# Pacing indirect transfers with a longer memset instead of tile gates, and a table that places the attention mix

## The reference

```python
x = x + 0.5 * ffn(layernorm(x))      # mixture of 8 experts, 2 chosen for each token
x = x + attention(layernorm(x))      # RWKV time mix: token shift, k, v, r, a scan over the sequence, Wo
x = x + 0.5 * ffn(layernorm(x))      # the same experts again
```

## Time and profile before

| | us |
|---|---|
| median of 3 runs | 674.68 (673.13 to 674.70) |
| the profiled execution | 672.78 |
| its span, first to last instruction | 671.0 |

### The profile page before, as it was taken

The page is one execution under the profiler, slowest core; times in us unless marked ns, Lnnn a source line. Parts: engine busy times, 40 slices in busy tenths (PEclk is TensorE's granted clock), DMA queues, the critical chain, the costliest instruction groups (busy, mean ns, idle before and its releaser), DMA issues. The chain is left out here.

```text
span 671.0 us, 18790 instructions
## 1 busy us (share of the span) xinstructions
PE 528.1 (79%) x5866; PEld 482.5 (72%) x5866; DVE 412.7 (62%) x1218; ACT 319.7 (48%) x703; POOL 297.2 (44%) x499
## 2 busy tenths in 40 slices
PE   2136899993899889898999859989789999989500
PEld 1125799893788878677888749878789899879500
DVE  4845975221678789588897848859786443333311
ACT  5433754441484566654656615854645344334100
POOL 1270356666540550565405655046005555525543
PEclk9999999998799999998999959999799999999955
DMA  8943234442221221222211133111112324322311
GB/s 287 325 143 99 84 112 147 136 134 67 76 77 41 64 72 49 73 64 63 78 49 45 53 99 83 44 60 49 57 34 77 100 81 127 85 64 72 86 52 43
DMA packets 89016, 59.57 MB, mean 89 GB/s; under 512 B 10208, under 2 KB 82656, under 8 KB 88928
## 3 DMA queue, kind: packets, MB, share of 16 engines
q1 hardware_dynamic: 55248, 29.97, 15.3%
q0 software_dynamic: 8192, 16.79, 8.9%
q10 hardware_dynamic: 25488, 11.61, 5.9%
HBM read 28.65 MB, written 29.69 MB: 87 GB/s over the span
## 5 line engine op out<-in xcount | busy, mean ns | idle before, releaser
L694 POOL DMA_INDIRECT rows_in<-parts,slot x128 | 132.5, 1035 | 232.9 <-DVE h L1084 136.4
L1084 DVE TENSOR_TENSOR h<-sil,pb 128x512 f32<-128x512 f32 x177 | 120.9, 686 | 145.8 <-PE pb L1201 59.3
L1215 PE MATMUL py<-ffn_w,h 128*128 x1416 | 199.0, 284 | 13.6 <-ACT yrow L753 12.4
L1215 PEld LDWEIGHTS py<-ffn_w,h 128*128 128x128 f32 x1416 | 175.3, 195 | 20.0 <-issue 13.9
L1201 PE MATMUL pa<-rT,ffn_w 128*128 128x128 f16 (+1 forms) x1752 | 152.7, 234 | 36.8 <-DVE h L1084 26.0
L708 POOL DMA_INDIRECT yg<-rows_out,slot x128 | 123.8, 968 | 130.3 <-issue 53.6
L1201 PEld LDWEIGHTS pa<-rT,ffn_w 128*128 x1752 | 124.9, 100 | 52.6 <-issue 41.1
L1201 PE MATMUL pb<-rT,ffn_w 128*128 128x128 f16 (+1 forms) x1752 | 157.1, 233 | 0.1
L1201 PEld LDWEIGHTS pb<-rT,ffn_w 128*128 x1752 | 124.4, 99 | 7.6 <-issue 0.3
L768 ACT ACTIVATE sil<-pa 128x512 f32<-128x512 f32 x177 | 105.4, 595 | 42.6 <-PE pa L1201 32.8
L748 ACT ACTIVATE rT<-pT 128x512 f16<-128x512 f16 (+1 forms) x112 | 56.8, 508 | 92.5 <-PE pT L1188 81.2
(11 more groups left out here) (155 smaller groups left out, 442.0 us busy)
## 6 DMA issues: line engine op xcount, KB each, us to landing
rows_out<-yrow ACTq DMA_DIRECT2D x177, 64.0 KB
rin<-rows_in SPq DMA_DIRECT2D x65, 128.0 KB
rows_in<-zrow SPq DMA_DIRECT2D x34, 128.0 KB
shared<-in_w SPq DMA_DIRECT2D x16, 256.0 KB, 7.0
rin<-rows_in SPq DMA_DIRECT2D x47, 64.0 KB
rows_in<-zrow SPq DMA_DIRECT2D x2, 1472.0 KB, 12.2
xres<-in_x SPq DMA_DIRECT2D x4, 512.0 KB, 5.7
ffn_w<-in_w SPq DMA_DIRECT2D x8, 256.0 KB
```

The costliest lines, as they stand in the source:

```text
L694: pool.indirect_dma_start(rows_in[g][:], bass.IndirectOffsetOnAxis(ap=slot[:, c, at:at + 1], axis=0), parts[:, at, :], None).then_inc(s_sc ...
L1084: dve.tensor_tensor(h[:, t % RING, :], sil[:, t % 2, :], pb[t % 2][:], ALU.mult).then_inc(s_h, 1)
L1215: mm = pe.matmul(py[:], h[:, step % RING, at:at + T], w, start=(c == 0), stop=(c == FC - 1))
```

## The change

1. **Pacing.** The list of transfers loses its gates (`s_h`). The memset behind each grows from 64 to 544 bytes a partition, into one of four buffers in turn; it waits only for the memset four transfers back, and the next transfer waits for no memset at all.
2. **Gather buffers by order.** `yg` has 3 buffers, used in the order of the gathers; a gather of unit n waits for the combine of the gather three before it.
3. **The last unit by blocks.** The 2 gathers of each of the last unit's 4 blocks have a semaphore of their own; DVE combines a block when both are there, and SP stores each block by itself.
4. **Placement.** The planner's costs change a little (`LAND` 4.0 to 4.5, `UP` 0.67 to 0.66 or 0.73, the slips), `SPACE` stays 1.6. A table `NOT_BEFORE` gives 36 steps a first tile, and `DUE_SHIFT` moves three due times.

```diff
-PACE = 64
+PACE = 544
+PACES = 4
+GSLOTS = 3
...
-HOP, LAND, SEND, LOAD = 0.1, 4.0, 1.1, 3.0
-SLIP = {"dve": 6.0, "act": 3.1, "pe": 2.0}
+HOP, LAND, SEND, LOAD = 0.1, 4.5, 1.1, 3.0
+SLIP = {"dve": 6.2, "act": 2.6, "pe": 2.0}
 SPACE = 1.6
+DUE_SHIFT = {
+    "stats6.1": -4, "combine2.0": -2, "stats5.0": 30
+}
+NOT_BEFORE = {
+    "stats2.0": 2, "pick21.0": 5, "hi2.0": 7, "rsqrt3.1": 7, "place21.0": 9, "hi3.1": 12, "xnT2.0": 12,
+    "pick22.0": 19, "scatter2.0": 23, "keep3.1": 27, "combine0.0": 35, "att0.0": 48, "v0.1": 48, "hi4.0": 59,
+    "xnT4.0": 61, "mstats1.1": 64, "count4.0": 66, "mnorm1.1": 68, "xT1.1": 71, "hi_m2.1": 90, "out2.0": 99,
+    "att2.1": 106, "combine3.0": 106, "mstats3.0": 107, "combine3.1": 112, "count6.0": 118, "turn_m3.1": 121,
+    "peak3.1": 126, "r3.1": 127, "exps3.1": 129, "scatter7.0": 133, "divide3.1": 134, "divide23.1": 135,
+    "stats8.0": 138, "turn8.0": 142, "combine4.1": 148, "combine5.0": 163
+}
...
-        if any(t is None for t in times):
+        if any(t is None for t in times) or tile < NOT_BEFORE.get(f'{step}{c.run}.{c.unit}', EARLY):
             return None
...
-            sp.wait_ge(s_out, 16 * B)
+            sp.wait_ge(s_out, 16 * (B - 1 + JU))
...
-                    before = [p[1:] for p in PLAN if p[1] == "gather" and p[3] == b]
-                    at_b = before.index(("gather", run, b))
-                    if at_b:
-                        pool.wait_ge(s_comb, count(("combine",), ("combine", before[at_b - 1][1], b)))
+                n = GATHERS.index((run, b))
+                if (j, c) == (0, 0) and n >= GSLOTS:
+                    pool.wait_ge(s_comb, count(("combine",), ("combine", *GATHERS[n - GSLOTS])))
...
-            for sent, (gate, name, *one) in enumerate(TRANSFERS):
-                wait(pool, s_h, gate)
-                wait(pool, s_pace, sent)
+            for sent, (_, name, *one) in enumerate(TRANSFERS):
                 if name == "scatter":
                     scatter(*one)
                 else:
                     gather(*one)
-                pool.memset(pace[:], 0).then_inc(s_pace, 1)
+                wait(pool, s_pace, sent - PACES + 1)
+                pool.memset(pace[:, sent % PACES, :], 0).then_inc(s_pace, 1)
...
+            def combine_last(run, b):
+
+                u, js = units(run, b)
+                slot_ = (len(GATHERS) - 1) % GSLOTS
+                for j in range(JU):
+                    xj = xres[:, js, :][:, j, :]
+                    dve.wait_ge(s_last[j], 16 * TOPK)
+                    for c in range(TOPK):
+                        ins = dve.scalar_tensor_tensor(xj, yg[:, slot_, c, j, :],
+                                                       wts[:, c, u * JU + j:u * JU + j + 1], xj, ALU.mult, ALU.add)
+                        if c == 0:
+                            link(ins)
+                    ins.then_inc(s_lastc, 1)
```

More of the change, by code:

```diff
@@ L157, in __init__ @@
     def __init__(self, steps, run, unit, due, start, follows=()):
-        self.steps, self.run, self.unit, self.due, self.start = steps, run, unit, due, start
+        self.steps, self.run, self.unit, self.start = steps, run, unit, start
+        self.due = (due[0] + DUE_SHIFT.get(f'{steps[0]}{run}.{unit}', 0),) + due[1:]
         self.follows, self.ends = list(follows), {}
@@ L187, in tile @@
         q, half, _ = TILE_OF[t]
-        up1 = max(self.free["pe"], self.rT[q] + HOP, self.h.get(t - 2, 0.0) + HOP) + UP
+        up = UP if paired(t) else UP_ALONE
+        up1 = max(self.free["pe"], self.rT[q] + HOP, self.h.get(t - 2, 0.0) + HOP) + up
         if t > SKEW:
@@ L191, in tile @@
         turned = self.turn(q + 1, up1) if t + 1 < TILES and TILE_OF[t + 1][1] == 0 else up1
-        up3 = turned + UP
+        up3 = turned + up
         silu = max(self.free["act"], up1 + HOP) + SILU
@@ L311, in ask, with in_use @@
         waiting.append([due, at, name, run, [(b, j, c) for b in units for j in range(JU) for c in range(TOPK)]])
+    def in_use(run, unit):
+        order = [p[2:] for p in plan if p[1] == "gather"]
+        n = order.index((run, unit))
+        return n >= GSLOTS and "combine" not in gathered[order[n - GSLOTS]].ends
     def send(tile, until):
         while True:
-            now = [w for w in waiting if w[1] <= until and not (w[2] == "gather" and any(
-                c.next() == "combine" for c in chains if c.unit == w[4][0][0] and gathered.get((c.run, c.unit)) is c
-                and c.run < w[3]))]
+            now = [w for w in waiting if w[1] <= until and not (w[2] == "gather" and in_use(w[3], w[4][0][0]))]
             at = max([free["pool"]] + [min((w[1] for w in now), default=until)])
@@ L385, in count @@
     return order.index(upto) + 1
+GATHERS = [p[2:] for p in PLAN if p[1] == "gather"]
 def run_of(t):
@@ L445, in macaron_kernel @@
         zrow = sb("zrow", [P, 2 * D], F16)
-        pace = sb("pace", [P, PACE], U8)
+        pace = sb("pace", [P, PACES, PACE], U8)
         e_desc = sb("e_desc", [P, JG, E])
@@ L490, in macaron_kernel @@
         yrow = sb("yrow", [P, YSLOTS, D])
-        yg = sb("yg", [P, UG, TOPK, JU, D])
+        yg = sb("yg", [P, GSLOTS, TOPK, JU, D])
         qkv_f = yg[:].rearrange("p b c j d -> p (b c j) d")[:, 0:6, :]
@@ L558, in macaron_kernel @@
         s_yst = [sem(f"y_stored{i}") for i in range(YSLOTS)]
-        s_gat = [sem(f"gathered{b}") for b in range(UG)]
+        s_gat = [sem(f"gathered{i}") for i in range(GSLOTS)]
+        s_last = [sem(f"last_gathered{j}") for j in range(JU)]
+        s_lastc = sem("last_combined")
         s_comb = sem("combined")
@@ L649, in step @@
                     u, js = units(run, b)
+                    if (run, b) == GATHERS[-1]:
+                        for j in range(JU):
+                            sp.wait_ge(s_lastc, j + 1)
+                            sp.dma_start(ov[:, js, :][:, j, :], xres[:, js, :][:, j, :]).then_inc(s_out, 16)
+                        return
                     sp.wait_ge(s_comb, count(("combine",), ("combine", run, b)))
@@ L702, in gather @@
                         pool.wait_ge(s_yst[k], 16 * len(range(k, PEND[run], YSLOTS)))
-                if (j, c) == (0, 0):
-                    before = [p[1:] for p in PLAN if p[1] == "gather" and p[3] == b]
-                    at_b = before.index(("gather", run, b))
-                    if at_b:
-                        pool.wait_ge(s_comb, count(("combine",), ("combine", before[at_b - 1][1], b)))
+                n = GATHERS.index((run, b))
+                if (j, c) == (0, 0) and n >= GSLOTS:
+                    pool.wait_ge(s_comb, count(("combine",), ("combine", *GATHERS[n - GSLOTS])))
                 pool.indirect_dma_start(
-                    yg[:, b, c, j, :], None, rows_out[SET[run]][0:PASS_STEPS[PASS[run]] * T, :],
-                    bass.IndirectOffsetOnAxis(ap=slot[:, c, at:at + 1], axis=0)).then_inc(s_gat[b], 16)
+                    yg[:, n % GSLOTS, c, j, :], None, rows_out[SET[run]][0:PASS_STEPS[PASS[run]] * T, :],
+                    bass.IndirectOffsetOnAxis(ap=slot[:, c, at:at + 1], axis=0)).then_inc(
+                        s_last[j] if n + 1 == len(GATHERS) else s_gat[n % GSLOTS], 16)
             def every(run, units):
@@ L1088, in combine @@
                 u, js = units(run, b)
-                runs = [p[2] for p in PLAN if p[1] == "gather" and p[3] == b]
-                dve.wait_ge(s_gat[b], 16 * TOPK * JU * (runs.index(run) + 1))
+                n = GATHERS.index((run, b))
+                dve.wait_ge(s_gat[n % GSLOTS], 16 * TOPK * JU * (n // GSLOTS + 1))
                 for c in range(TOPK):
@@ L1093, in combine @@
                         xj = xres[:, js, :][:, j, :]
-                        ins = dve.scalar_tensor_tensor(xj, yg[:, b, c, j, :], wts[:, c, u * JU + j:u * JU + j + 1],
-                                                       xj, ALU.mult, ALU.add)
+                        ins = dve.scalar_tensor_tensor(xj, yg[:, n % GSLOTS, c, j, :],
+                                                       wts[:, c, u * JU + j:u * JU + j + 1], xj, ALU.mult, ALU.add)
                     if c == 0:
@@ L1106, in step @@
                 if name == "combine":
-                    combine(run, b)
+                    (combine_last if (run, b) == GATHERS[-1] else combine)(run, b)
                 if name in ("stats", "mstats"):
```

2 lines of the change are left out of this document (1 added, 1 removed).

## The result

The changed kernel takes 626.87 us in the median of 4 runs (625.27 to 627.24), beside 674.69 for the kernel before on the same chip: a ratio of 0.929 (95% interval 0.926 to 0.931), 47.8 us less. The profiled execution took 627.05 us, its span 625.2, so 45.8 us less than the span before. The forecast was 641, the range 626 to 668: the sign was right, the gain was four tenths larger than the sum, and the time lies 0.9 us inside the lower edge of the range.

A forecast was written before the change was run, and what follows sets the result against it. The prediction took POOL's transfer spacing to bound the first combine and the end. Its terms (-11.5, -2, -1.5, -2.5, -2, -4, -10.0) summed to -33.5 us: 639.3 profiled, 641.2 against the median; range 626 to 668.

The forecast's parts named there:

- Spacing: POOL's paced transfers: without the wait for the memset they start 1.75 us apart, with a memset of 0.44 to 0.54 us.
- The gates: Tile gates on POOL's transfers: hardly binding; 1 to 3 us at the tail, 1.2 counted in the tail's spacing.
- The first combine: DVE's 13.1 us wait at the combine of run 0, unit 0 falls to about 1.6: -11.5 us.
- What is late next: Run 2's rows, ready at 186.4 and needed at 188: covered with 2 us to spare, but not at spacing 1.9.
- Other waits in the body and run 5: Gather waits in the body -1.5, -2.5 and -2 us; PE's 4.08 us wait for run 5's rows, -4 us.
- The tables at 0, 8 either way: Table moves of mix and routing steps remove no instruction: counted at 0, possibly 8 us either way.
- The tail: From run 6's first gather: spacing -8.0 us, fewer combines behind the last gather -1.6, smaller store -0.4; together -10.0.
- (3): Rival: spacing above the tiles' rate, POOL falls behind everywhere; at 2.4 us +19, so 694; chance 0.10.
- (2): Rival: the memset hides in the issue, spacing 1.4 us; -49.5 us, so 625; chance 0.10.
- (1): Rival: the body gives less, transfers stretched to a mean of 1.9 us; -17, so 657.7; chance 0.22.
- (4): Rival: held-back table steps come due together before runs 4 to 7, DVE stalls PE; +30, about 675; chance 0.10.
- (5): Rival: the longer memset delays DVE's single-input mix instructions; 3.4 us, at most 12: 645 to 653; chance 0.08.

The follow-up runs named there:

- run 6: Not a follow-up run but a stretch of the kernel's own work; its first gather starts at 601.76 us in the kernel before. It has no measured time or ratio.

## Why the prediction was right, and where its terms were off

The places named, the first combine, the waits in the body, run 5 and the tail, are those where the time was won, and the lead cause, POOL's spacing, is the right one. The size of the whole is not: the sum was 33.5 us, measured were 47.8. That the range holds the time, by 0.9 us, is luck. Its lower end stood for a memset hidden in the issue, at 1.4 us of spacing, and that did not come.

*Spacing*: 1.75 forecast, 1.69 measured. The memset took 573 ns (forecast 0.44 to 0.54 us, by a line through three short ones), the gap ahead of a transfer 0.16 us and not 0.30. The two errors partly cancel.

*The gates*: put at 1.2 us; in the changed kernel they cost 13. This was the worst step. It read the gates' price from a plan in which they stood close to their data (0.9 us behind it at run 5), and carried it to a plan in which they stand up to 9.95 us behind. What the gates cost in the order before, no run shows: pacing alone takes away gates, spacing and the wait for the memset together.

*The first combine*: -11.5 forecast, -2 more for the clock and -1.5 for the second combine; both waits and the low clock are gone, and the stretches from tile 34 to 46 give 17.2 together. The reason given, the order of the list, is one of two that nearly suffice: the order with the old pacing leaves a wait of 4.3 us, the new pacing with the old order 1.7.

*What is late next*: run 2's rows were to be ready with 2 us to spare at 1.75 and late at 1.9. They never were late in a kernel without gates, not even at 1.88. The step took the scatters to start at tile 23, since the table says so; they started at 119.17, as soon as their slots were made. In the changed kernel with the old pacing they were 0.7 us late.

*Other waits in the body and run 5*: -6 and -4 forecast. The three groups of 3.0, 5.6 and 9.2 us went altogether; at run 5 PE still waits 1.30 us of 4.08. The stretches from tile 46 to run 6's first gather gave 18.0 us, where the terms for it came to 8.5.

*The tables at 0, 8 either way*: under the new pacing they are worth 3 to 5 us, within it. The costs beside them weren't priced at all, and they are worth 11 where no tables are; with the tables they were not tried. Their size is that of the 13 us not accounted for, and so is the gates'; prices taken out of one finished kernel overlap and don't add up, so how the 13 us divide stays open. A planner's constants are a change of the order like any table.

*The tail*: 31 steps -8.0 forecast, -9.5 measured. The 2.0 us for the last unit's blocks were nought: the sum let the last combine and its store end the span, but POOL's `DRAIN` ends it, 10.4 us from the last gather and not some 8.

*The rivals.* (3), slower by wider spacing, did not come. Its slope is about right near 1.8 us: 87 us for each us forecast, 20 us for 0.19 (105) measured between 1.69 and 1.88, but 35 between 1.49 and 1.69. (2) took spacing below 1.5 for a free gain; at 1.49 it is 7 us, and at 1.39 the sign turns. No case of the prediction had that. (1) and (4) did not come: the body gave more than the sum, not less, and the tables cost nothing. (In (4), 30 us on the forecast make 671, not the 675 written; and 671 or 675 lies outside the range too, which the account of the range leaves out.) (5) came true as a mechanism. One of DVE's three single-input steps of the mix, by form (count, busy us, mean ns, idle before), in the changed kernel, and with 770 bytes:

```profile
L1179 DVE TENSOR_SCALAR shared<-shared,wdec 128x512 f32<-128x512 f32 x8 | 6.1, 764 | 0.1
```
```profile
L1179 DVE TENSOR_SCALAR shared<-shared,wdec 128x512 f32<-128x512 f32 x8 | 7.5, 944 | 0.1
```

496 ns before, 764 with the longer memset, 944 with the longest. The three forms of the mix rose by 5.2 us together (3.4 forecast) and DVE's busy time as a whole from 412.7 to 423.6 us, nearly all of it in `TENSOR_SCALAR` and `CAST`; `h` stayed at 686 and 685 ns, and the scan of two SBUF inputs at 1218 and 1216. This agrees with the Trainium skill, "SBUF — State Buffer" (section "Who interferes with whom"): a GpSimd instruction that only writes leaves a DVE instruction with two SBUF inputs alone, while one in a 2-port mode and it exclude each other. That these steps run in a 2-port mode no row shows. How much of the gain the 11 us of DVE's time ate, no run tells.

The same section of the Trainium skill says that a DMA never contends with a compute engine. By the expectation for 64 bytes, if the spacing counts as time on POOL alone, the kernel should have taken 617 us; measured are 871, with the other engines nearly at a stand. The rows show semaphore updates that come late and matmuls held up without a wait. What holds them up, the data, their descriptors, the semaphores or something else, is open: nothing tried here tells these apart.

## What to carry to other kernels

Price a pacing by what the next stage needs by when, not by its time on the issuing engine, and try two or three spacings on both sides, for the best one may lie a tenth of a microsecond from a step. A gate that looks cheap in one order can cost much in the next; if the data's own semaphores keep the order right, leave it out. Before shortening the last unit's work, check in two kernels whether the end of the span moves with it at all.

## What the runs showed of the hardware

Indirect transfers issued by POOL with a memset of 184 bytes or less between them, 1.39 us apart or less, bring PE, ACT and DVE nearly to a stand while tiles run beside them: a burst of 16 holds one to three tiles at 1.29 us (871 us in all) and two to six at 1.39 (822 us), against 8 at 1.49, which does no such harm (620 us). The 16 scatters of run 0, 1.26 to 1.31 us apart with no memset between and no tiles beside them, held up nothing that was seen. POOL's `DRAIN` at the end of the program ended 10.2 us, and the span 10.4 us, after the start of the last indirect transfer in all fourteen kernels of this study. A memset on POOL takes 169, 269, 371, 466, 573 and 758 ns for 64, 184, 304, 416, 544 and 770 bytes a partition. One of DVE's `TENSOR_SCALAR` steps of 128x512 took 496 ns on average beside the short memset and 764 when a memset ran 0.57 us in each 1.69.
